# A CIN recommender tower: layer 0's shifts regrouped so that two steps load in one transfer, with edits at the start and the tail

## The reference

```python
e = jnp.stack([tbl_0[ids[:, 0]], ..., tbl_38[ids[:, 38]]], axis=1)     # (512, 39, 16)
prev = x = e
for k in range(3):                                                     # 128 units each
    z = jnp.einsum('bmd,bhd->bdmh', x, prev).reshape(b, D, m * h)
    t = jnp.einsum('bdc,co->bdo', z, ws[k]) + bs[k]
    t = jnp.transpose(t, (0, 2, 1))
    t = t / jnp.sqrt(jnp.sum(t * t, axis=(-2, -1), keepdims=True))
    logit.append(t)
    prev = t
z = jnp.sum(jnp.concatenate(logit, axis=1), axis=-1)
h = jnp.concatenate([z, dense_ctx], axis=1)
h = jnp.maximum(h @ W_top1 + b_top1, 0.0)
h = jnp.maximum(h @ W_top2 + b_top2, 0.0)
y = h @ W_top3
```

## Time and profile before

| | us |
|---|---|
| median of 3 runs | 1181.57 |
| the three runs | 1180.67, 1181.57, 4874.38 |
| the profiled execution | 1181.07 |
| its span | 1179.2 |
| TensorE / VectorE / GpSimd / ScalarE busy | 1124.8 / 972.1 / 868.3 / 126.4 |
| DMA traffic | 204.31 MB in 104409 packets |

### The profile page before, as it was taken

One profiled execution on the slowest core, in us unless ns is written; L12 is line 12 of the kernel. 1 busy time (PEld: TensorE's weight loads), 2 busy tenths in 40 slices (PEclk: granted clock), 3 DMA queues, 4 the chain that ended last, 5 costly groups with the idle time before them and its releaser, 6 DMA issues. The chain is left out here.

```text
span 1179.2 us, 21810 instructions
## 1 busy us (share of the span) xinstructions
PE 1124.8 (95%) x7868; PEld 568.1 (48%) x7868; DVE 972.1 (82%) x836; ACT 126.4 (11%) x266; POOL 868.3 (74%) x614
## 2 busy tenths in 40 slices
PE   0789999999999999999999999999999999999999
PEld 0344445455444545544454554545455454545553
DVE  1678889889898988988898898989889898988782
ACT  0000110101011010101101011110101011010102
POOL 5567768788786878877686886868788786856670
PEclk9889999999999999999999999999999999999999
DMA  5958446382744638274463837546382845637010
GB/s 163 382 150 277 142 165 211 98 294 68 286 131 162 210 96 299 68 280 136 144 220 97 306 68 263 154 167 208 95 296 68 282 134 176 211 104 274 1 47 1
DMA packets 104409, 204.31 MB, mean 173 GB/s; under 512 B 49131, under 2 KB 52075, under 8 KB 104390
## 3 DMA queue, kind: packets, MB, share of 16 engines
q1 hardware_dynamic: 97610, 202.52, 51.9%
q0 software_dynamic: 5120, 1.29, 1.1%
q10 hardware_dynamic: 1660, 0.25, 0.2%
HBM read 201.72 MB, written 2.30 MB: 173 GB/s over the span
## 5 line engine op out<-in xcount | busy, mean ns | idle before, releaser
L560 DVE TENSOR_TENSOR z<-t_ps,xb 128x2048 f32<-128x2048 f32 (+1 forms) x352 | 708.1, 2042 | 97.6 <-PE acc L711 73.8
L281 POOL TENSOR_TENSOR sums<-z,sums 128x1024 f32<-128x1024 f32 x192 | 455.4, 2372 | 15.1
L697 PE MATMUL acc<-z,w_sb 128*64 128x512 f32 x1920 | 436.5, 598 | 12.5 <-DVE z L560 12.5
L278 POOL TENSOR_TENSOR sums<-z 128x512 f32<-128x512 f32 x192 | 245.2, 1277 | 193.0 <-DVE z L560 189.2
L711 PE MATMUL mix_ps<-sums,s_sb 128*64 128x256 f32 x1536 | 282.6, 380 | 6.0 <-POOL sums L281 6.0
L697 PEld LDWEIGHTS acc<-z,w_sb 128*64 128x64 f32 x1920 | 137.8, 138 | 246.8 <-issue 224.8
L711 PE MATMUL acc<-z,w_sb 128*64 128x256 f32 x768 | 228.4, 379 | 0.0
L711 PE MATMUL mix_ps<-z,w_sb 128*64 128x256 f32 x768 | 228.4, 379 | 0.0
L711 PE MATMUL acc<-z,s_sb 128*64 128x256 f32 x768 | 228.4, 379 | 0.0
L711 PE MATMUL p_ps<-z,w_sb 128*64 128x256 f32 x768 | 228.4, 379 | 0.0
L711 PEld LDWEIGHTS mix_ps<-sums,s_sb 128*64 128x64 f32 x1536 | 158.8, 137 | 93.6 <-POOL sums L281 13.1
(11 more groups left out here) (76 smaller groups left out, 404.9 us busy)
## 6 DMA issues: line engine op xcount, KB each, us to landing
xb<-xt SPq DMA_DIRECT2D x80, 768.0 KB, 6.8
xb<-xq SPq DMA_DIRECT2D x96, 512.0 KB, 4.7
xb<-xt SPq DMA_DIRECT2D x96, 512.0 KB, 6.3
xr<-xt SPq DMA_DIRECT2D x144, 156.0 KB
x<-xt SPq DMA_DIRECT2D x45, 78.0 KB
gathered<-in_table,rows_of POOLq DMA_INDIRECT x160
xr<-xt SPq DMA_DIRECT2D x32, 78.0 KB
xt<-gathered SPq DMA_DIRECT2D x16, 72.0 KB, 2.3
```

What stands on the lines that cost most here:

```text
L278: nc.gpsimd.tensor_tensor(t2, t3, b11, ALU.add).then_inc(sums_ready, 1)
L281: nc.gpsimd.tensor_tensor(t41, b2, t2_twice, ALU.subtract).then_inc(sums_ready, 1)
L560: nc.vector.tensor_tensor(z[:, at:at + n, :], t_ps[k - 1][:, :].rearrange("p (a n) -> p a n", a=1).broadcast_to([P, n, N]), xb[:, XB_ROW[c ...
L697: last = nc.tensor.matmul(acc[k][o, :], w_sb[k][:, field + r, o], z[:, at + r, :], start=(c == 0 and r == 0), stop=(c == NCH - 1 and r == ...
```

## The change

1. Layer 0's shifts are dealt differently: step k now holds the shifts k, k+7 and k+14 (the last step 6 and 13), so that steps k and k+1 of one stack slot are neighbouring rows of `xt`. A group of two steps becomes one transfer: outermost the 3 shifts (7 rows apart), then 39 rows, then 4 KB in one piece (two neighbouring rows); on the other side 117 partitions. The last group has 2 shifts against 78 partitions. x3 is one transfer too, the source repeated three times. load_layer0 issues 5 transfers instead of 14. For tile 0, ScalarE's queue issues x3 and groups 1 and 3, SyncE's groups 0 and 2.
2. The rows are written in another order: the last gather has a semaphore of its own, three of the four writes wait for the first nine gathers only.
3. The masks are two columns, broadcast, with a semaphore of their own; the index add no longer waits for them.
4. Layer 2's mixed weights are built in four parts behind chunks 7 to 10 of tile 0's layer 1. The three functions around it are written more generally; shapes stay as they are.
5. At the first and the last norm the sum of squares comes before the sum over d, which goes to another PSUM bank.
6. The dense rows lie on four row groups (partitions 0, 32, 64, 96), one per block of 128 units, and their four matmuls come together behind the others. Eight small loads instead of two; the clearing of the pads moves one pair chunk earlier.
7. w0's symmetric sum is one add instead of two.

```diff
-SHIFT_OF = [[PER_STEP * k + j + 1 for j in range(PER_STEP)] for k in range(STEPS0 - 1)] + [[SHIFTS - 1, 0]]
+SHIFT_OF = [[k + STEPS0 * j for j in range(PER_STEP) if k + STEPS0 * j < SHIFTS] for k in range(STEPS0)]
...
+        def load_x(engine, i):
+            blk = xt[bass.ds(i, 1), :, :].rearrange("a m n -> (a m) n")
+            src = bass.AP(blk.tensor, blk.offset, [[0, PER_STEP], [N, FIELDS], [1, N]])
+            engine.dma_start(x3[:, :], src).then_inc(x3_loaded, 16)
+
+        def load_shifted(engine, i, g):
+            k0, k1 = LOADS0[g]
+            shifts = len(SHIFT_OF[k1 - 1])
+            blk = xt[bass.ds(i, 1), :, :].rearrange("a m n -> (a m) n")
+            src = bass.AP(blk.tensor, blk.offset + k0 * N, [[STEPS0 * N, shifts], [N, FIELDS], [1, (k1 - k0) * N]])
+            engine.dma_start(xr[0:shifts * FIELDS, k0:k1, :].rearrange("p k n -> p (k n)"),
+                             src).then_inc(xr_loaded[g], 16)
...
-            pool.wait_ge(ids_loaded, 48)
+            pool.wait_ge(ids_loaded, 32)
...
-                        if k == 2 and c == FIRST_P + 1 and last:
+                        if k == 2 and c == PADS_AT and last:
...
+                full, rest = divmod(SHIFTS - 1, GROUP)
+                sp.wait_ge(rows_gathered, 16 * (GROUPS - 1) * (i + 1))
+                write(0, 0, GROUPS - 1)
+                write(FIELDS, 0, full)
+                write(FIELDS + full * GROUP, full, full + 1, rest)
+                sp.wait_ge(last_gathered, 16 * (i + 1))
+                write((GROUPS - 1) * GROUP, GROUPS - 1, GROUPS, LAST_GROUP)
...
-            load_layer0(0, with_x3=False)
+
+            load_shifted(sp, 0, 0)
+            load_shifted(sp, 0, 2)
...
+            load_x(act, 0)
+            load_shifted(act, 0, 1)
+            load_shifted(act, 0, 3)
...
-                    if c == 6 and first:
-                        mixed_weights(2)
+                    if c >= NCH - 4 and first:
+                        mixed_weights(2, c - NCH + 4)
...
-            norm_sums(0, 0)
-            normalize(0, 0, 1)
+            sum_squares(0, 0)
+            sum_d(0, 0, dsum_alone)
+            normalize(0, 0, 1, dsum_alone)
...
-                nc.tensor.matmul(h1_ps[j][:, :], wt1d_sb[:, o], dense_sb[:, :], start=False, stop=False)
+
+            for j in range(TOP1 // P):
+                r = slice(j * DENSE_AT, (j + 1) * DENSE_AT)
+                nc.tensor.matmul(h1_ps[j][:, :], wt1d_sb[r, :], dense_sb[r, :], start=False, stop=False)
```

More of the change, by code:

```diff
@@ L51 @@
 PAIR_GROUPS = 3
-PAIRED = 2 * GROUP * PAIR_GROUPS
-PAIRS = PAIRED // 2
+PAIRS = GROUP * PAIR_GROUPS
 PLAIN_IN = [3, 3, 0, 0, 3, 0, 0, 3, 0, 0, 3]
 def chunks():
-    out, field, p = [], PAIRED, 0
+    out, field, p = [], 2 * PAIRS, 0
     for n in PLAIN_IN:
@@ L68, with chunk_of @@
 XB_ROW = [sum(n for _, _, n in CHUNKS[:c]) for c in range(NCH + 1)]
+def chunk_of(row):
+    return next(c for c in range(NCH) if XB_ROW[c + 1] > row)
+PADS_AT = next(c for c in range(chunk_of(4), NCH) if CHUNKS[c][0] == "P")
 FIRST_P = PLAIN_IN.index(0)
@@ L90 @@
 SUM_SLOTS = 2
+QUADS = [q for q in ((0, PAIRS // GROUP, GROUP), (PAIRS // GROUP, 1, PAIRS % GROUP)) if q[2]]
 LEFT, RIGHT = slice(0, UNITS // 2), slice(UNITS // 2, UNITS)
@@ L97 @@
 DENSE = 16
+DENSE_AT = 32
 def pair_fields(p):
@@ L317, in write_rows, with write @@
             def write_rows(i):
[L319 to L326, removed]
+                def write(first, g0, g1, fields=GROUP):
+                    blk = xt[bass.ds(i, 1), first:first + (g1 - g0 - 1) * GROUP + fields, :].rearrange(
+                        "a (g f) (b d) -> (a f b) g d", f=fields, d=EMB)
+                    sp.dma_start(blk, gathered[0:fields * TILE_B, g0:g1, :]).then_inc(xt_written, 16)
+                full, rest = divmod(SHIFTS - 1, GROUP)
[5 more added lines that the diff above has]
+                write((GROUPS - 1) * GROUP, GROUPS - 1, GROUPS, LAST_GROUP)
             def write_mixed(i):
@@ L332, in write_mixed, with load_layer0 @@
                              mixed[:, :, :]).then_inc(xq_written, 16)
[L334 to L346, removed]
+            def load_layer0(i):
+                load_x(sp, i)
+                for g in range(len(LOADS0)):
+                    load_shifted(sp, i, g)
             def load_rows(c, blk, first, rows, at):
@@ L515, in by_sample, with mixed_weights @@
                 return x.rearrange("p (b d) -> p b d", d=EMB)
-            def mixed_weights(k):
-                pairs = w_sb[k][:, 0:PAIRED, :].rearrange("p (q s j) o -> p q s j o", s=2, j=GROUP)
-                a11, a21 = pairs[:, :, 0, :, LEFT], pairs[:, :, 0, :, RIGHT]
-                a12, a22 = pairs[:, :, 1, :, LEFT], pairs[:, :, 1, :, RIGHT]
-                s1, s2, s4 = (s_sb[k][:, r, :, :].rearrange("p (q j) o -> p q j o", j=GROUP) for r in range(3))
-                dve.wait_ge(w_loaded[k], 16)
-                nc.vector.tensor_tensor(s1, a21, a22, ALU.add).then_inc(s_step[k], 1)
-                dve.wait_ge(s_step[k], 1)
-                nc.vector.tensor_tensor(s2, s1, a11, ALU.subtract).then_inc(s_step[k], 1)
-                dve.wait_ge(s_step[k], 2)
-                nc.vector.tensor_tensor(s4, a12, s2, ALU.subtract).then_inc(s_step[k], 1)
-                nc.vector.tensor_tensor(a21, a11, a21, ALU.subtract).then_inc(s_step[k], 1)
+            def mixed_weights(k, part):
+                for q, groups, count in QUADS:
+                    rows = w_sb[k][:, 2 * GROUP * q:2 * GROUP * (q + groups), :].rearrange(
+                        "p (q s j) o -> p q s j o", s=2, j=GROUP)
+                    a11, a21 = rows[:, :, 0, 0:count, LEFT], rows[:, :, 0, 0:count, RIGHT]
+                    a12, a22 = rows[:, :, 1, 0:count, LEFT], rows[:, :, 1, 0:count, RIGHT]
+                    mine = slice(GROUP * q, GROUP * q + groups * count)
+                    s1, s2, s4 = (s_sb[k][:, r, mine, :].rearrange("p (q j) o -> p q j o", j=count) for r in range(3))
+                    if part:
+                        dve.wait_ge(s_step[k], part * len(QUADS))
+                    else:
+                        dve.wait_ge(w_loaded[k], 16)
+                    out_, x, y, op = [(s1, a21, a22, ALU.add), (s2, s1, a11, ALU.subtract),
+                                      (s4, a12, s2, ALU.subtract), (a21, a11, a21, ALU.subtract)][part]
+                    nc.vector.tensor_tensor(out_, x, y, op).then_inc(s_step[k], 1)
             def products0(i, groups):
                 if at_first(i):
-                    dve.wait_ge(x3_loaded, 16 * PER_STEP)
+                    dve.wait_ge(x3_loaded, 16)
                     x = x3[:, :]
```

105 lines of the change are left out of this document (61 added, 44 removed).

## The result

| | us |
|---|---|
| before, median of 4 runs | 1181.12 |
| changed kernel, median of 4 runs (1300.62 to 1303.59) | 1302.92 |
| ratio, 95% interval | 1.1029 (1.1008 to 1.1051) |
| its profiled execution; span | 1303.59; 1301.7 |

The change costs 122 us: 10% slower, where 1254.3 was forecast. The span is 122.5 us longer than before's 1179.2. I split it at two marks, the first matmul of layer 2 in tile 0 and in the last tile: the start is 33.2 longer (126.74 against 93.56), the fifteen intervals between the marks 90.6 (1118.8 against 1028.2), the tail 1.3 shorter (56.2 against 57.5).

What follows compares the result with a forecast made beforehand. TensorE, busy 1124.8 of 1179.2 us, was taken as the bound. 1181.1 + 19.8 (start) + 6.0 (GpSimd) + 49.0 (waits before layer 2) - 1.6 (tail) = 1254.3 us; own range 1215 to 1310, whole range 1195 to 1320.

Steps and rivals of the forecast that it cites:

- rival C: Middle tiles: loads narrow and each TensorE wait also drops the clock, 14 x 2.7 us more, 1292 us; chance 0.11.
- the price of a narrow load: Layer 0 loads: first engine carries 639 kB per tile, 25.1 us at 25.4 kB/us, 35.4 at worst.
- Rival A: Layer 0 loads spread over 13 or more engines after all, middle tiles stay at 70 us: 1171.2 us; chance 0.11.
- Rival B: Loads narrow but middle tiles covered, ready times 3 us better, only the start paid: 1199.3 us; chance 0.06.
- My 3.5 sits at the latter: Middle tiles: the 3.5 us TensorE wait leaves the clock at 1.00, as 3.5 us idle in the last tile did.
- the wait, 3.5: Middle tiles: TensorE waits 510.6 - 507.1 = 3.5 us before layer 2 for VectorE; 14 tiles make 49.0 us.
- the tile, 70 us: Middle tiles before the change: each lasts as long as its matmuls, 70 us, read from a fully busy 70 us stretch.
- the 0.4 for GpSimd, 6.0 in all: Layer 2 started hungry: TensorE later waits another 0.4 us for GpSimd; 15 x 0.4 = 6.0 us.
- the first engine's time at the start: Start: serial work of 56.6 us lands w2 at 78.7, layer 2 of tile 0 at 113.4: +19.8 us, bounds +10 to +30.
- Layer 0 of tile 0 itself comes 11 to 19 us late, inside that: Start: tile 0's layer 0 delay of 11 to 19 us is hidden within the +19.8 us.
- The start edits: Start, if loads stay wide: 2.5 us earlier loads, 1.3 for sums, 7.5 for w2's wait and half clock less about 3.
- Tail: Last tile: dense matmuls overlapping on row groups -2.6 us, pads cleared earlier on GpSimd +0.95, sum -1.6.

Runs made afterwards that it cites:

- wide_all: The changed kernel with every layer 0 load split by shift again (14 transfers per tile), all other edits kept: 1174.74 us, ratio to before 0.9943.
- x3_last_wide: The changed kernel with x3 and the last group split by shift, groups 0 to 2 left narrow: 1220.48 us, ratio to before 1.0332.
- x3_wide: The changed kernel with x3 alone split in three transfers again, the groups left narrow: 1257.0 us, ratio to before 1.0636.
- narrow_only: The kernel before with only the new dealing of shifts and one transfer per group: 1303.41 us, ratio to before 1.1042.
- start_wide: The changed kernel with the loads of tiles 0 and 1 alone split by shift, tiles 2 to 15 narrow: 1269.03 us, ratio to before 1.0742.
- first_narrow: The changed kernel with only tile 0's five loads narrow, all later tiles' loads split by shift: 1195.28 us, ratio to before 1.0110.
- wide_early: wide_all with layer 2's mixed weights made in one piece behind chunk 6 of tile 0 again: 1174.22 us, ratio to before 0.9939.

## Why the prediction was right, and where it was wrong

The measured time, 1302.9 us, lies in the stated range but 48.6 above the number, near the range's upper end: the range was wide enough for it because it took in rival C and a microsecond of error per tile.

**Right: the direction, the mechanism, and the price of a narrow load.** Three engines per load (two for the last), 25.1 us for the first engine's share: the last group came 27.6 us behind the issue on average, 26.8 were predicted. VectorE's products, the shared sums behind them, TensorE's wait before layer 2: each in its place, in every tile. Rival A (wide) was excluded by three completion packets per load, and wide_all shows what it would have been, 1174.7 where I had put 1171.2. Rival B (covered) fell with 69.5 us of waits.

**Wrong: the clock.** My step was "My 3.5 sits at the latter", the wait that leaves the clock at 1.00. Rival C, which had 0.11, is what happened: 14 tiles, each with 24 matmuls in 7.64 to 8.12 instead of 5.32 us, about 14 x 2.5 = 35 us, and 1.8 more in tile 0. C's number, 1292, was nearer than mine. The row that I leaned on proves little: the same wait of the last tile, 3.53 us, left full clock in the kernel before and half clock in the one with only the new dealing:

```profile
1121.50 8.29 PE L697 MATMUL acc<-z,w_sb 128*64 128x512 f32 x24 [3.53 <-DVE z L560]
```

All 14 kernels of this document have that wait of 3.52 or 3.53 us in the last tile, and in ten of them half clock followed; before was one of the four where it did not. One row of a wait with the clock still up is not a bound. What the middle tiles support is: at 0.1 to 0.9 us never (x3_last_wide), at 2.2 to 2.6 in 6 of 14 (x3_wide), at 3.3 to 4.5 in all (the changed kernel, narrow_only, start_wide).

**Missized: the wait, 3.5.** It measured 58 us in 14 tiles (69.5 less 4.2, 3.7 and 3.5 us of tiles 0 and 15), 4.15 each: 9 us more than my 49.0. The last group came 0.8 us later than predicted, and the wait is 0.65 longer.

**Missized: the tile, 70 us.** I took a window of 70 us with TensorE always busy for the length of a tile. Undisturbed tiles take 68.27 (163.28 to 231.54 in wide_all). A window shows that nothing waits, not how long the period is; this changed no term of the sum.

**Wrong: the 0.4 for GpSimd, 6.0 in all.** After a wait that leaves the clock up it does come (0.44 in x3_wide, in the eight tiles at full clock and in none of the six at half). In the changed kernel TensorE starts layer 2 at half clock and GpSimd has time: 0 in the middle tiles. Apart from this, the three long intervals of before, 6.6 us in all, are gone. The clock does not explain that, since narrow_only has half clock and still has them; they went with the standing gathers. That gain I had not seen. Against my sum the two are 6.0 + 6.6 = 12.6 less, and this luck covers a third of what the clock cost.

**Missized: the first engine's time at the start.** The step was "the serial work of the first engine: layer 0 25.1, a sixteenth of xb's 10.2 MB at 25.4 kB/us 25.2, a sixteenth of w2 6.3", 56.6 us in all. w2 landed at 91.2 and not at 78.7. From the first load at 22.1 that is 69.1 us for the same 1.44 MB, 20.8 kB/us and not 25.4. The rate came from a stretch of before without narrow loads, in which the median 4 KB packet took 159 ns; in the changed kernel it took 219 ns between 24 and 42. The rest of the chain held: tile 1's loads went out 1.5 us behind w2, at 92.68 (80.2 predicted), and layer 2 of tile 0 began at 126.74 (113.4). GpSimd's mixed rows did not hold them up, being ready at 83.1, 7.8 us before SyncE wrote them:

```profile
82.82 0.28 POOL L295 TENSOR_TENSOR mixed<-mixed,masked 128x48 f32<-128x48 f32 x1
```

So the start cost 33.2 us and not 19.8, past the end of its bounds, 30. A second chain was nearly as long, and the prediction had it too short: "Layer 0 of tile 0 itself comes 11 to 19 us late, inside that". It came 28.5 us late, and first_narrow, with tile 1's loads wide, shows that this alone delays layer 2 of tile 0 by 20.6 us.

**The start edits.** I had counted 2.5 us of earlier loads, 1.3 of sums and 7.5 for w2's wait less 3 under rival A. The loads did go out sooner (21.77 against 23.59), but in wide_all layer 2 of tile 0 starts 1 us later than before. Between 24 and 66 the DMA engines are saturated there (every slice at 80% or more), which would explain that an earlier issue brings nothing forward, and wide_early shows the mixed weights' place to be worth nothing that can be told.

**Tail: right within 0.3.** -1.3 measured, -1.6 predicted: 2.4 from the row groups, and a wait of 1.32 us for GpSimd where 0.43 was. The Trainium skill's sentence that tiles run in parallel ("TensorEngine Tiling (Array Packing)", section "Key Properties") agrees with the 1.07 us above; of a drain that takes the gain back no row shows anything.

The sum: the start is 13.4 above its term (33.2 for 19.8), the tail 0.3, and the middle 35.6 (90.6 for 49.0 + 6.0): 1254.3 + 13.4 + 0.3 + 35.6 = 1303.6, the profiled execution. The middle is made of 58.1 us of waits, 35.3 of half clock and 1.8 more in tile 0, less the 6.6 of before's three intervals; 88.6 so far. The other 2.0 fit the end of layer 0: from its start to the start of the wait TensorE takes 6.19 us, where in before layer 2 follows after 6.02, and 14 x 0.17 = 2.4. The half clock has no part in it, as it ends inside the first 24 matmuls in every tile. Errors of both signs are in the number: the clock, the waits and the start made it too low, and 12.6 us of GpSimd's waits worked the other way.

## What to carry to other kernels

Before merging transfers, look at the outermost counts of both sides: merging by stacking a short dimension in front turned 13 engines into 3, and putting the long one first kept the merge and the engines. The merge itself brought nothing that can be told. And price a recurring TensorE wait with the clock drop behind it, unless waits of its length are seen with full clock many times: here the single row that said so was the exception.

## What the runs showed that I had not expected

- Waits of nearly the same length have both outcomes: 2.57 us with full clock and 2.44 with half in one execution, 3.53 with either in two kernels.
- An engine that issues into full queues is held (4.68 us in one issue), and freeing it made the kernel 7.9 us slower (1310.8 against 1302.9): w2, issued 10.9 us sooner, landed no sooner, and the rows that were needed first came 18.8 us later (84.70 against 65.92).
- Edits can depend on each other's cover: the row groups gained 2.4 us of TensorE time in both kernels, but in the one without the earlier sum of squares a wait of 0.99 us took some of it back.
- The rate of an engine is not one number: the median 4 KB packet took 219 ns where narrow loads met xb's (24 to 42), and 159 ns in before's saturated stretch.
